# GNN on one core: the output addition of the attention stage one step later, gathers ahead from the third group, and two tiles scattered early for the last eighteen chunks

## The reference

```python
# first layer: attention over the edges (and a loop edge for each node), 4 heads of 32
x_l = (x @ W_l + b_l);  x_r = (x @ W_r + b_r)
m = leaky_relu(x_l[s] + x_r[d], 0.2)
e = einsum(m, att)                                   # a score per edge and head
alpha = exp(e - seg_max[d]) / segment_sum(exp(e - seg_max[d]), d)
out = segment_sum(alpha * x_l[s], d) + bias
# second layer: filters from the edges' attributes
Wij = (ssp(f_ij @ Wf1 + bf1) @ Wf2 + bf2) * rcut_ij
agg = segment_sum((x @ W_in2f)[src] * Wij, dst)
out = ssp(agg @ Wo1 + bo1) @ Wo2 + bo2
```

## Time and profile before

| what | value |
|---|---|
| median of 3 runs | 3022.98 us (3020.04 to 3025.41) |
| the profiled execution | 3014.57 us |
| its span | 3012.7 us |
| mean granted clock of TensorE | 0.93 |
| busy: PE, DVE, ACT, POOL | 79%, 75%, 64%, 63% of the span |
| DMA moved | 593.04 MB |

### The profile page before, as it was taken

One profiled execution on the slowest core, in us unless ns is written; L12 is line 12 of the kernel. 1 busy time (PEld: TensorE's weight loads), 2 busy tenths in 40 slices (PEclk: granted clock), 3 DMA queues, 4 the chain that ended last, 5 costly groups with the idle time before them and its releaser, 6 DMA issues. The chain is left out here.

```text
span 3012.7 us, 59625 instructions
## 1 busy us (share of the span) xinstructions
PE 2392.7 (79%) x16506; PEld 1659.0 (55%) x16506; DVE 2267.1 (75%) x6293; ACT 1939.7 (64%) x4383; POOL 1908.9 (63%) x1650
## 2 busy tenths in 40 slices
PE   5888997998899998997677777777777777488777
PEld 4666664344444444445555555555555555377777
DVE  7777875688888878876787777777787787366666
ACT  5878886766666666660555555555555555289887
POOL 2677776377777777742588888888888888600000
PEclk9999998999999999996899899999899899789998
DMA  7999995266566655554566666666655656689998
GB/s 224 299 310 326 287 292 189 84 192 188 179 211 191 192 189 188 179 171 130 113 117 119 111 117 113 119 113 117 119 112 115 124 113 123 173 322 425 426 426 338
DMA packets 390076, 593.04 MB, mean 197 GB/s; under 512 B 148151, under 2 KB 225323, under 8 KB 364818
## 3 DMA queue, kind: packets, MB, share of 16 engines
q1 hardware_dynamic: 291682, 479.21, 48.4%
q0 software_dynamic: 98288, 112.65, 19.0%
HBM read 353.86 MB, written 246.47 MB: 199 GB/s over the span
## 5 line engine op out<-in xcount | busy, mean ns | idle before, releaser
L736 POOL DMA_INDIRECT sum_dram<-b_sum,b_at x392 | 636.9, 1625 | 148.5 <-issue 119.4
L650 POOL DMA_INDIRECT a_xs<-in_x,index x320 | 331.5, 1036 | 108.1 <-issue 98.9
L657 POOL DMA_INDIRECT a_xd<-in_x,index x320 | 328.7, 1027 | 97.5 <-issue 87.5
L724 POOL DMA_INDIRECT x_dram<-b_xo,sidx x294 | 312.7, 1064 | 105.1 <-issue 90.6
L1666 PE MATMUL bank<-b_rows,b_same 128*128 128x128 bf16 x4704 | 307.5, 231 | 0.6 <-ACT b_sum L1434 0.6
L1666 PEld LDWEIGHTS bank<-b_rows,b_same 128*128 128x128 bf16 x4704 | 292.6, 104 | 0.6 <-issue 0.6
L1275 ACT ACTIVATE d_n<-d_x,stat_d_shift,stat_d_rstd 128x128 f32<-128x128 f32 x686 | 283.5, 486 | 0.2 <-DVE stat_d_shift L772 0.2
L1699 PE MATMUL bank<-wo,f_ssp_out 128*128 128x128 f32 x1568 | 228.1, 292 | 63.1 <-DVE f_ssp_out L1221 61.5
L1699 PEld LDWEIGHTS bank<-wo,f_ssp_out 128*128 128x128 f32 x1568 | 204.4, 203 | 80.1 <-DVE f_ssp_out L1221 73.8
L1481 PE MATMUL bank<-ident,d_n 128*128 128x128 f32 x1184 | 193.2, 289 | 67.3 <-DMA d_n<-sum_dram 38.0
L1527 PE MATMUL bank<-wl,turned 128*128 128x128 f32 x1568 | 234.9, 295 | 10.8 <-ACT turned L1272 9.5
(11 more groups left out here) (234 smaller groups left out, 6138.8 us busy)
## 6 DMA issues: line engine op xcount, KB each, us to landing
d_x<-in_x SPq DMA_DIRECT2D x196, 256.0 KB
x_dram<-d_x SPq DMA_DIRECT2D x196, 256.0 KB
out<-d_x SPq DMA_DIRECT2D x49, 1024.0 KB, 10.1
sum_dram<-zero SPq DMA_DIRECT2D x48, 1024.0 KB
d_x<-x_dram SPq DMA_DIRECT2D x45, 1024.0 KB, 14.2
d_n<-sum_dram SPq DMA_DIRECT2D x25, 1024.0 KB, 11.9
a_beta<-beta_dram SPq DMA_DIRECT2D x392, 64.0 KB
x_end_dram<-a_xo SPq DMA_DIRECT2D x98, 256.0 KB, 3.0
```

The source lines that it names most:

```text
L650: pool.indirect_dma_start(a_xs[t % DEPTH][:, j * F:(j + 1) * F], None, x, column(t, j)).then_inc(gathered[t % GSEM], 16)
L657: pool.indirect_dma_start(a_xd[t % DEPTH][:, j * F:(j + 1) * F], None, x, column(t, TILES + j)).then_inc(gathered[t % GSEM], 16)
L724: pool.indirect_dma_start(x1_dram, bass.IndirectOffsetOnAxis(ap=sidx[s][:, j:j + 1], axis=0), b_xo[s][:, j * F:(j + 1) * F], None, bounds_ ...
L736: pool.indirect_dma_start(sum_dram, bass.IndirectOffsetOnAxis(ap=b_at[s][:, j:j + 1], axis=0), b_sum[s][:, j * F:(j + 1) * F], None, compu ...
```

## The change

It has three parts. (1) STAGED goes from 18 to 21; the gathers ahead may begin when `d_x1_ready` is 12 and not 20, and their thresholds spread over two groups more. The turning of the index lists on TensorE, which the gathers need, goes two groups forward, and so do the helper steps on VectorE. (2) VectorE's output addition `a_xo` of a chunk goes from the end of its own step to a place right behind the next step's scan; the loop has one step more; the wait for the scan before (`sum_scan`) stands ahead of `a_gate`. (3) For the last LAST = 18 chunks two tiles and not one are scattered in stage A, and so the first 18 chunks of stage B scatter two tiles and not three; the loops of B are cut there, and the counts waited for follow.

```diff
-STAGED = 18
+STAGED = 21
+LAST = 18
+LAST_EARLY = 2
...
+        def early_of(c):
+            return LAST_EARLY if c >= NC - LAST else EARLY[c % 2]
...
+        def scattered_b(k, u, later):
+            s = u % 2
+            few = 16 * (TILES - LAST_EARLY)
+            many = 16 * (TILES - EARLY[1 - s])
+            if not later:
+                return few * turn(k, u)
+            return many * turn(k, u) - (many - few) * (LAST // 2)
...
-                for j in range(EARLY[s]):
+                for j in range(early_of(t)):
                     pool.indirect_dma_start(x1_dram, column(t, 2 * TILES + j), a_xo[t % 4][:, j * F:(j + 1) * F], None,
...
-                done = QUADS * (RX + 1) + n * QUADS * (NG - RX - 3) // len(ahead)
+                done = QUADS * (RX - 1) + n * QUADS * (NG - RX - 1) // len(ahead)
                 pool.wait_ge(d_x1_ready, done)
...
-                for j in range(EARLY[1 - s], TILES):
+                for j in range(EARLY[1 - s] if later else LAST_EARLY, TILES):
                     pool.indirect_dma_start(x1_dram, bass.IndirectOffsetOnAxis(ap=sidx[s][:, j:j + 1], axis=0),
...
-            with pool.Fori(2, HALF) as k:
+            with pool.Fori(2, LAST // 2) as k:
                 for u in range(2):
-                    scatters(k, u)
+                    scatters(k, u, False)
+                    adds(k, u - 2)
+            with pool.Fori(LAST // 2, HALF) as k:
+                for u in range(2):
+                    scatters(k, u, True)
                     adds(k, u - 2)
...
-            beside = (output_bias, edge_lists, edge_weights, index_columns)
+            beside = (output_bias, edge_lists, index_columns, edge_weights)
...
+                    if c >= 1:
+                        dve.wait_ge(sum_scan, c)
                     dve.scalar_tensor_tensor(out=a_gate[:, :], in0=a_beta[s][:, :], scalar=-1.0, in1=a_keep[s][:, :],
...
                     dve.tensor_tensor_scan(a_o[s][:, :], a_gate[:, :], a_pv[:, :], a_o[1 - s][:, C - 1:C] if c else 0.0,
                                            ALU.mult, ALU.add).then_inc(sum_scan, 1)
+                c = t - LAG - 1
+                if 0 <= c < NC:
+                    s = c % 2
+                    dve.wait_ge(out_turned, c + 1)
+                    if c >= 4:
+                        dve.wait_ge(end_stored[s], 16 * ((c - 4) // 2 + 1))
+                        dve.wait_ge(early_scattered[s], 16 * early_upto(c - 4))
+                    dve.tensor_tensor(a_xo[c % 4][:, :], bank[6 + s][:, :], a_xd[c % DEPTH][:, :], ALU.add).then_inc(x1_ready, 1)
...
-                if back:
-                    dve.wait_ge(out_turned, c + 1)
...
-                    dve.tensor_tensor(a_xo[c % 4][:, :], bank[6 + c % 2][:, :], a_xd[c % DEPTH][:, :], ALU.add).then_inc(x1_ready, 1)
...
-            for t in range(NC + LAG):
+            for t in range(NC + LAG + 1):
                 step_a(t)
...
+                if g == 1:
+                    turn_lists()
                 if g == 2:
-                    turn_lists()
-            turn_last_list()
+                    turn_last_list()
```

More of the change, by code:

```diff
@@ L339, in early, with early_upto @@
             return EARLY[s] * F
-        def late(s):
-            return 16 * (TILES - EARLY[1 - s])
+        def early_of(c):
+            return LAST_EARLY if c >= NC - LAST else EARLY[c % 2]
+        def early_upto(c):
+            return sum(early_of(i) for i in range(c % 2, c + 1, 2))
+        def scattered_b(k, u, later):
[5 more added lines that the diff above has]
+            return many * turn(k, u) - (many - few) * (LAST // 2)
         def node_rows(a, g):
@@ L492, in load_rows_b @@
                 if t0 >= 2:
-                    sp.wait_ge(x1_scattered[s], late(s) * turn(k, u - 2))
+                    sp.wait_ge(x1_scattered[s], scattered_b(k, u - 2, later))
                     sp.sem_inc(sync_step, 1)
@@ L500, in load_rows_b, with step_b @@
                              attr_dram[bass.ds((NC - 1 - t) * C, C), :].rearrange("(j p) r -> p j r", p=P)).then_inc(b_fa_ld[s], 16)
-            def step_b(k, u, t0, ahead=True):
+            def step_b(k, u, t0, ahead=True, later=True):
                 s = u % 2
@@ L716, in _, with scatters @@
             pool.wait_ge(cleared, 16 * NG)
-            def scatters(k, u):
+            def scatters(k, u, later):
                 s = u % 2
@@ L1393, in norms_b @@
                 if t0 >= 2:
-                    act.wait_ge(x1_scattered[s], late(s) * turn(k, u - 2))
+                    act.wait_ge(x1_scattered[s], scattered_b(k, u - 2, later))
                 act.activation(b_xo[s][:, early(1 - s):], b_x[s][:, early(1 - s):], ACT.Copy).then_inc(b_xo_ready, 1)
@@ L1402, in norms_b, with step_b @@
                 last.then_inc(b_norm, 1)
-            def step_b(k, u, t0, ahead=True, front=True, mid=True, back=True):
+            def step_b(k, u, t0, ahead=True, front=True, mid=True, back=True, later=True):
                 s = u % 2
@@ L1435, in step_b @@
                 if ahead:
-                    norms_b(k, u + 1, t0 + 1)
+                    norms_b(k, u + 1, t0 + 1, later)
             act.wait_ge(ones_set, 1)
             inverse_deviation(act, stat_e[0], TILES, b_var, b_logv, b_rstd, 1)
-            norms_b(0, 0, 0)
+            norms_b(0, 0, 0, later=False)
             for u in range(4):
-                step_b(0, u, u, mid=u >= 1, back=u >= 2)
-            with act.Fori(2, HALF - 1) as k:
+                step_b(0, u, u, mid=u >= 1, back=u >= 2, later=False)
+            with act.Fori(2, LAST // 2) as k:
+                for u in range(2):
+                    step_b(k, u, 4 + u, later=False)
+            step_b(LAST // 2, 0, 4, later=False)
+            step_b(LAST // 2, 1, 5)
+            with act.Fori(LAST // 2 + 1, HALF - 1) as k:
                 for u in range(2):
```

32 lines of the change are left out of this document (16 added, 16 removed).

## The result

The changed kernel is slower: 3028.86 us (median of 19 runs) beside 3019.61 (19 runs of the kernel before), a ratio of 1.0027 with a 95% interval from 1.0016 to 1.0037, that is 5 to 11 us. The forecast was 7.6 us less than before, within 3004 to 3026.

What follows compares the result with a forecast made beforehand. DMA was taken to bound stage D, a ring of TensorE, VectorE and ScalarE stage A, GpSimd stage B. +2.4 + 9.6 - 6 + 1.4 - 15 = -7.6, so 3015.4 us beside the median before, range 3004 to 3026.

Steps and rivals of the forecast that it cites:

- Stage D: Part 1: three more staged chunks lengthen groups during staging, 9.27 us against 8.87; +2.4 us, bounds 0 and 10.
- Steady steps: Stage A, part 2: the addition ahead of the shift delays ScalarE in even steps; +9.6 us, bounds 0 and 25.
- two kinds: Stage A's even steps: 20 set by ScalarE lose 0.42 us each, 18 where TensorE is late lose 0.05.
- so I put nothing down for them: Stage A's odd steps: same VectorE instructions between a_u and the next a_dif, so no loss was counted.
- all three have slack there: Stage A: early scatters, SP's last-row store and gathers behind them can take x1_ready a step later; no cost counted.
- The tail: End of stage A: VectorE stops waiting for TensorE's turn, eleven rounds at about 4.8 us, not 5.4; -6, range 0 to -9.
- What is late next is SP's load of a_keep: Tail rounds: this load, estimated 4.3 us, or TensorE at up to 4.65 sets the round; gain 0 if always the load.
- 3.1 us of its own work: Tail of stage A: what remains of VectorE's round once it no longer waits for TensorE's turn.
- Boundary: Stage A to B: only the last added scatter stands on the path, a GpSimd scatter with its gap; +1.4 us.
- Stage B: Part 3: 15 chunks each save 1.36 us of GpSimd less 0.35 for landing waits; -15 us, range 0 to -20.4.
- the rival: Stage B: additions landing 4 us or later make the removed scatter only uncover a wait; B gains 0, 3030 us; chance 0.10.
- four rivals: Landing as new wait (0.10), shift costs nothing (0.20), DMA full in stage D (0.13), shift's whole 0.6 counts (0.04).

Runs made afterwards that it cites:

- e1: The changed kernel with the gathers left in stage A spread over 76 steps and not 80: ratio 0.9977 to the kernel before, 3018.47 us.
- e13: The kernel before with part 2 alone and stage A's gathers spread over 76 steps: ratio 1.0012, 3029.06 us.
- e7: The changed kernel with stage A's gathers over 76 steps and SP's store of x1 one step later: ratio 0.9941 to the kernel before, 3005.67 us.
- e8: The kernel before with parts 1 and 3, the addition late only from step 98 on, and SP's store one step later: ratio 0.9908, 2997.72 us.
- e11: e8 with three tiles, not two, of the last 18 chunks scattered in stage A: ratio 0.9935 to the kernel before, 3001.53 us.

## Why the prediction was wrong

**Stage D (+2.4, measured -0.2; alone 0.9994).** The mechanism that the text names is there: in all seventeen profiles the groups are longer while chunks are staged (9.05 to 9.50 us, then 8.51 to 8.88), and with 21 chunks the staging ends at 308.5 to 313.9 in place of 293.3 to 301.2. But the stage as a whole doesn't get longer: its last addition is at 478.9 as a mean of the twelve kernels with 21 staged and at 479.8 in the five with 18. Its end moves by 10 us from one profile to the next, and what makes up for the 2.4 stays open.

**Steady steps (+9.6, measured +11.2 up to step 84; 8 to 12 in the kernels with the late addition).** The kernel before has the lowest of nine values there; by the means the loss is 8.9 us, all of it from step 14 on, as the first additions come in steps 12 and 13. The mechanism of the shift is right with its two kinds, and its size a third too large: 18 of the 42 even steps at 0.33 are 6 us. The step "so I put nothing down for them", said of the odd steps, failed: six of their seven kinds lose 0.14, 36 steps and 5 us, since the addition no longer covers the end of the statistics. The sum came out close because two errors met, which is luck. That ScalarE waits for the rows of the carry too was not in the sum; what these waits cost can't be told from the spread of the two kinds with most rows.

**The last gathers (nothing, measured +15.4).** This is the step that decided. Forecast and profile lie 24.5 us apart (-7.6 and +16.9), of which 15.4 are here and 6.4 in the tail. The prediction says of the early scatters, SP's store and the gathers behind them that "all three have slack there (GpSimd 58 of 75 us busy)". Two things are wrong in it. A busy share says nothing on how many steps lie between a scatter and the instruction that needs what is queued behind it; that margin is read from the order of both engines, and it went from two steps to one and none. And the 58 us were read without the 54 gaps of 0.30 that the same text counts in stage B: with them GpSimd is at 74 of 75, in that window (from 600 to 1345 it still waited 17 us for additions), and around step 91 it lost 3.77 us in a wait and hadn't made them up 26 us later. `e1` and `e13` show that margin is enough to cure it. `e1` then comes out where the forecast was (0.9977 beside 0.9975), but that is luck: its tail gains nothing, and in its profile chunks 3 to 18 of B gain 11.4 us where the steps of A lose 11.0.

**The tail (-6, measured +0.4).** That VectorE would be free of TensorE's turn was right. "What is late next is SP's load of a_keep", put at 4.3 a round, was the right name with the wrong size: as the store waits for an addition that now comes behind the next scan, the rounds stay at 5.5 us as a mean (60.2 / 11), in the last six of them between 3.1 and 7.6. The bound of 0 that the text names is what came. With the queue free (`e7`, `e8`) they take 4.5 us as a mean, less than the 4.8 of the forecast, and the gain is 10 to 11 us: the "3.1 us of its own work" was right for the last six rounds, and the text put an even 4.8 on all eleven. The tail of the kernel before isn't one number either. Its last six rounds take 5.4 us where TensorE's turn takes 2.08, at a granted clock of 0.50 (the level of 1.2 GHz), and 4.5 where it takes 1.16, with the clock at 0.88 to 1.00 (2.4 GHz for all or most of it); by how many are of which kind, the tails of kernels with the addition at its old place are 59.8 to 61.7 us, and a change of 0.4 can't be told from nothing.

**Boundary (+1.4, measured +2.2, and 1.4 more up to b_msg 3).** Chunks 96 and 97 have their last additions at 1453.54 and 1454.87, one right behind the other, so four scatters follow each other from 1455.11 to 1459.9, where the text counted one more. The 1.4 up to b_msg 3 are not always there: of the thirteen kernels with part 3 five have them, and eight take 27.6 to 28.1 us like the kernel before; no run says why.

**Stage B (-15, measured -12.2; -9.3 by the means of all profiles).** Right in kind and 3 to 6 us too large. A chunk has 1.36 us less of scatters and gets 0.6 to 0.8 shorter; the rest, 0.55 to 0.74, comes back as waits for landings. The term that was mis-sized is the 0.35 put for these. It doesn't follow from the text's own counts either: 18 gaps at 0.5 and 7 at 1.3 are 18 us, and over 95 gaps that is 0.19 a chunk. The landing of at most 3.3 us as a mean (`e11`) is below the 4.0 from which the rival would have decided; two scatters with their gaps (2 x 1.36 + 0.30 = 3.0) end ahead of it, and three ended behind it. By the fit in the Trainium skill (DMA: Bandwidth & Descriptors, "Anatomy of one DMA — SWDGE (gpsimd) path") a DMA of 64 KB would take an estimated 2.15 us. No run here has such a DMA alone; the last of four in a row takes longer, and the rows decide.

None of the four rivals was the case, though the landing took back half of part 3's saving. The one that the text needed, a transfer issued too late behind a wait that was moved, was named in the list of what the change touches and given no price.

What stays open: stage D, the later part of stage B and stage F differ by 7 to 10 us from one profile to the next in kernels that are alike there, and no run says why. The steadier stretches (the steps of A up to 84, the tail, chunks 3 to 18 of B) repeat to 2 to 4 us, and only the mean of several kernels reads them closer; the span of one profile can't be read so.

## What to carry to other kernels

When an instruction that raises a semaphore is moved a step later, list every queue in which something waits for it, and for what stands behind each waiting instruction count the steps to its own user; a busy share can't answer this. In the tail, a wait removed on one engine was worth something only when the next one, here a store ahead of loads in one queue, was moved as well. An independent instruction between a producer and its user on the same engine covers the producer's end, and moving it away costs that cover. And where two profiles of one kernel differ by 3 us in a stage, take the size of a term from all kernels that are alike there.

## What the runs showed of the hardware

A sum on VectorE that needs the four statistics ahead of it starts 0.88 us after the last of them starts, an addition that doesn't need them 0.77 after. Four accumulating scatters of 64 KB from GpSimd had landed 3.3 us or less after the last one's end, as a mean of 15 chunks (`e11`). One scatter less in a chunk of stage B takes 1.36 us off GpSimd; the chunk got 0.6 us shorter with the step from three to two (means of four and twelve kernels) and 0.7 with the step from two to one (`e11` beside the twelve), and the rest came back as waits for landings. TensorE's turn of a chunk (eight matmuls of 128x128, f32) took 2.08 us at a granted clock of 0.50 and 1.16 at 1.00.
